# An expert's token tiles turned by VectorE in 32x32 blocks, after a load in 128-byte pieces, in place of two TensorE transposes

## The reference, cut to what matters

```
xn = layernorm(x)
# 1: attention over tokens (16 heads of 16 channels), then over channels
qk = (layernorm(xn, ln1) @ Wqk_t) in 16 heads;  v = ... @ Wv_t
attn = softmax(tau * (2 qk.qk' - |qk|^2 - |qk'|^2) / sqrt(16));  out = (attn @ v) @ Wo_t * gamma1
...                                   # channel attention on the result
# 2: a mixture of 8 experts, the best one for each token
h = relu(xn @ W1[e] + b1[e]);  y = h @ W2[e] + b2[e];  out = gate * y
result = x + (1) + (2)
```

## The kernel before, in words

| round | expert work on TensorE | name below |
|---|---|---|
| 0 | two transposes of the tile (x) | x round |
| 5, 10 | two transposes of the next tile, two last products with W2 of the one before | x+y round |
| 1, 6, 11 | two columns of h (W1 products), L1134 | h round |
| 2-4, 7-9, 12-14 | two columns of h, two products with W2 (y), L1118 | h+y round |
| 15 | two last products with W2 | y round |

## Time and profile before

### The profile page before, as it was taken

One profiled execution on the slowest core, in us unless ns is written; L12 is line 12 of the kernel. 1 busy time (PEld: TensorE's weight loads), 2 busy tenths in 40 slices (PEclk: granted clock), 3 DMA queues, 4 the chain that ended last, 5 costly groups with the idle time before them and its releaser, 6 DMA issues. The chain is left out here.

```text
span 1476.7 us, 27029 instructions
## 1 busy us (share of the span) xinstructions
PE 1391.3 (94%) x9041; PEld 663.7 (45%) x9041; DVE 403.0 (27%) x1009; ACT 1064.6 (72%) x1183; POOL 232.2 (16%) x314
## 2 busy tenths in 40 slices
PE   6997999999999999999999999999999999999978
PEld 4752222234444444444444444344444444444867
DVE  6872110011111211112111111111121111123977
ACT  4657999987777777777777777777777777775122
POOL 5210730001001000010010100100001001001870
PEclk9998999999999999999999999999999999999989
DMA  4686442724543626345454454353544645532423
GB/s 165 232 239 215 127 89 54 224 37 115 157 112 123 145 85 170 98 110 167 104 163 114 110 155 116 130 127 87 154 122 105 171 104 157 136 133 84 152 89 115
DMA packets 125321, 195.38 MB, mean 132 GB/s; under 512 B 22336, under 2 KB 91648, under 8 KB 121824
## 3 DMA queue, kind: packets, MB, share of 16 engines
q1 hardware_dynamic: 116240, 177.12, 44.0%
q0 software_dynamic: 9040, 17.71, 4.4%
HBM read 154.63 MB, written 35.95 MB: 129 GB/s over the span
## 5 line engine op out<-in xcount | busy, mean ns | idle before, releaser
L939 ACT ACTIVATE shared<-ps 128x1024 f32<-128x1024 f32 x1024 | 980.5, 1024 | 264.8 <-PE ps L1076 263.8
L1091 PE MATMUL ps<-shared,work 128*17 128x512 f32 x4096 | 505.6, 603 | 0.0
L1076 PE MATMUL ps<-mov,stat 52*128 52x512 f32 x2048 | 423.7, 465 | 51.3 <-ACT shared L939 37.4
L1076 PEld LDWEIGHTS ps<-mov,stat 52*128 52x128 f32 x2048 | 167.5, 185 | 428.4 <-ACT shared L939 402.4
L984 DVE TENSOR_SCALAR work<-ps,work 128x128 f32<-128x128 f32 x312 | 109.6, 351 | 587.2 <-PE ps L1134 572.3
L1091 PEld LDWEIGHTS ps<-shared,work 128*17 128x17 f32 x4096 | 90.1, 97 | 220.8 <-issue 199.2
L1134 PE MATMUL ps<-work,XNW 128*128 128x128 f32 x1248 | 180.7, 288 | 0.0
L1134 PEld LDWEIGHTS ps<-work,XNW 128*128 128x128 f32 x1248 | 151.0, 191 | 57.0 <-issue 57.0
L1118 PE MATMUL ps<-XNW,work 128*128 128x256 f32 x624 | 161.8, 382 | 0.0
L788 POOL DMA_DIRECT2D y_slots<-work x39 | 21.9, 562 | 701.2 <-DVE work L976 642.2
L1118 PEld LDWEIGHTS ps<-XNW,work 128*128 128x128 f32 x624 | 106.5, 191 | 12.8 <-issue 4.8
(11 more groups left out here) (170 smaller groups left out, 689.7 us busy)
## 6 DMA issues: line engine op xcount, KB each, us to landing
XNW<-in_L_ffn_W_dram SPq DMA_DIRECT2D x78, 1024.0 KB, 7.1
stat<-q_parts SPq DMA_DIRECT2D x192, 128.0 KB
mov<-q_parts SPq DMA_DIRECT2D x192, 64.0 KB
xg<-in_L_attn_x_dram SPq DMA_DIRECT2D x16, 512.0 KB, 4.9
q_parts<-XNW SPq DMA_DIRECT2D x16, 512.0 KB, 5.8
x_slots<-work SPq DMA_DIRECT2D x1, 4992.0 KB, 16.4
early<-x_slots SPq DMA_DIRECT2D x39, 128.0 KB, 2.2
early<-in_L_ffn_b_dram SPq DMA_DIRECT2D x39, 128.0 KB, 8.1
```

Source lines behind the costliest of these rows:

```text
L939: nc.scalar.activation(probs[:, s % DEEP, half * 1024:(half + 1) * 1024], ps[:, 2 * half:2 * half + 2].rearrange("p a b -> p (a b)"), ACT. ...
L1076: last = nc.tensor.matmul(ps[:, 2 * half + r], stat[rows, hh, m * P:(m + 1) * P], mov[rows, hh, half * 512:(half + 1) * 512], start=True, ...
L1091: last = nc.tensor.matmul(ps[32 * j:32 * j + VW, AV], Vh[:, hh, m], probs[:, s % DEEP, j * 512:(j + 1) * 512], start=(m == 0), stop=(m == ...
```

## The change

The tokens of a tile are no longer loaded as 128 rows of 1024 bytes. Four DMAs take them in pieces of 32 fp32 (128 bytes): DMA a fills the partitions 32a to 32a+31, and it picks the channels so that a transpose of each 32x32 block by itself gives the full transpose of the tile. This block transpose is one VectorE instruction on 128x256, from `xs` to `xsT`, both in SBUF. The two transposes on TensorE and the two copies on VectorE are gone, with their two uses of the ring: the pair now has 24 of these, not 30. A new semaphore `x_turned` tells TensorE that `xsT` is there, in front of the first h columns, and the wait on `tile_loaded` moves there as well; VectorE waits on `tile_loaded` too. A tile now takes 8 DMAs on SP's queue, not 5.

```diff
-        TILE_DMAS = 5
+        TILE_DMAS = 8
+        QUADS = 4
+        QUAD = P // QUADS
...
-                rounds[at] += [("x", tt, 0), ("x", tt, 1)]
+                rounds[at].append(("x", tt, 0))
...
-                    get(xs[:, tt], x_slots[bass.ds(n * P, P), :])
+                    rows = x_slots[bass.ds(n * P, P), :].rearrange("(t c) (k a r) -> a c k t r", c=QUAD, k=KC, r=QUAD)
+                    for a in range(QUADS):
+                        get(xs[a * QUAD:(a + 1) * QUAD, tt].rearrange("c (k t r) -> c k t r", k=KC, t=QUADS), rows[a])
...
+                            elif kind == "x":
+                                dve.wait_ge(tile_loaded[a], 16 * TILE_DMAS * (i - FIRST + 1))
+                                nc.vector.transpose(xsT[:, a].rearrange("p c n -> p (c n)"), xs[:, a]).then_inc(x_turned, 1)
...
-                                if kind == "x":
-                                    nc.vector.tensor_copy(xsT[:, a, b], ps[:, bank(k), 0:P]).then_inc(ring_taken, 1)
...
+                    if kind == "x":
+                        return
                     k = use[u]
                     at_least(pe, ring_taken, ring_base(i) + k - 1)
-                    if kind == "x":
-                        if b == 0:
-                            pe.wait_ge(tile_loaded[a], 16 * TILE_DMAS * (i - FIRST + 1))
-                        nc.tensor.transpose(ps[:, bank(k), 0:P], xs[:, a, b * P:(b + 1) * P],
-                                            ident[:, :]).then_inc(ring_ready, 1)
-                    else:
-                        if b == 0:
-                            pe.wait_ge(ring_taken, ring_base(i) + use[("x", a, 1)] + 1)
...
+                    if b == 0:
+                        pe.wait_ge(tile_loaded[a], 16 * TILE_DMAS * (i - FIRST + 1))
+                        pe.wait_ge(x_turned, 3 * (i - FIRST) + a + 1)
```

More of the change, by code:

```diff
@@ L738, in build @@
         ring_taken = sem("ring_taken")
+        x_turned = sem("x_turned")
         y_ready = sem("y_ready")
@@ L744, in ring_base @@
         def ring_base(i):
-            return 30 * (i - FIRST)
+            return 24 * (i - FIRST)
         def expert_plan():
@@ L762, in use_numbers @@
                 for u in uses:
-                    if u[0] != "y":
+                    if u[0] == "h":
                         table[u] = k
@@ L980, in expert_body @@
                                 dve.wait_ge(ring_ready, ring_base(i) + k + 1)
-                                if kind == "x":
-                                    nc.vector.tensor_copy(xsT[:, a, b], ps[:, bank(k), 0:P]).then_inc(ring_taken, 1)
-                                else:
-                                    nc.vector.tensor_scalar(hT[:, b], ps[:, bank(k), 0:P], b1s[:, a, b:b + 1], 0.0,
-                                                            ALU.add, ALU.max).then_inc(ring_taken, 1)
+                                nc.vector.tensor_scalar(hT[:, b], ps[:, bank(k), 0:P], b1s[:, a, b:b + 1], 0.0,
+                                                        ALU.add, ALU.max).then_inc(ring_taken, 1)
                         if n == 0:
@@ L1122, in expert @@
                         return
+                    if kind == "x":
+                        return
                     k = use[u]
                     at_least(pe, ring_taken, ring_base(i) + k - 1)
-                    if kind == "x":
-                        if b == 0:
-                            pe.wait_ge(tile_loaded[a], 16 * TILE_DMAS * (i - FIRST + 1))
-                        nc.tensor.transpose(ps[:, bank(k), 0:P], xs[:, a, b * P:(b + 1) * P],
-                                            ident[:, :]).then_inc(ring_ready, 1)
-                    else:
-                        if b == 0:
-                            pe.wait_ge(ring_taken, ring_base(i) + use[("x", a, 1)] + 1)
[L1133 to L1136, removed]
+                    if b == 0:
+                        pe.wait_ge(tile_loaded[a], 16 * TILE_DMAS * (i - FIRST + 1))
+                        pe.wait_ge(x_turned, 3 * (i - FIRST) + a + 1)
+                    for c in range(KC):
+                        last = nc.tensor.matmul(ps[:, bank(k), 0:P], w1s[:, a, c, b * P:(b + 1) * P],
+                                                xsT[:, a, c], start=(c == 0), stop=(c == KC - 1))
+                    last.then_inc(ring_ready, 1)
                 def expert_body(i, last_one=False):
```

## The result

The changed kernel takes 1481.42 us (median of 12 runs, 1478.39 to 1483.71), the kernel before 1477.94 us (12 runs on the same chip, 1475.30 to 1479.13). The ratio is 1.0027, with an interval of 1.0018 to 1.0036: slower by about 0.27%; the medians are 3.5 us apart. The time is within the range, but the likeliest case, 1479 us with no added falls of the clock, did not come. What came is the first rival, between its small size (1 to 3 more falls) and its full one (six), together with a gain that stood in no case.

A forecast was written before the change was run, and what follows sets the result against it. Light rounds were taken as bound by the chain of logits and ScalarE's exponentials, not TensorE; TensorE, VectorE, waits, DMAs and clock each added 0 to 1478.41 us, giving 1479 us, range 1476 to 1489.

The forecast's parts named there:

- the likeliest case: Whole kernel: removed TensorE work is off the path and no clock falls are added; 1479 us, chance 0.53.
- the first rival: In x rounds, less TensorE work makes the clock fall more often: about 1483 us to 1488.5 us; chance 0.39.
- the clock term: In x rounds of the expert pairs: 0 more clock falls, cost 0; up to nine more, 14.8 us, kept for the range.
- The bound of the light rounds: In x, y, h and x+y rounds, logits and ScalarE's exponentials set the length, about 4.8 us; removing transposes gains 0.
- the 17.2 us: TensorE's transposes in 13 x and 26 x+y rounds, 39 x 0.44 us, all predicted to be off the path.
- One of its signs: In the profile after, TensorE's busy time would be down by about 17 us at the same span.
- VectorE and the new wait: Block transposes of 0.43 us replace VectorE's copies, and TensorE's wait for `x_turned` in rounds 1, 6, 11 is covered; cost 0.
- The DMAs: Three more SP issues per tile and tokens landing in 5 us stay within 26 us of slack; cost 0.
- the doubled allowance: On SP's queue, loads going out 0.8 to 1.3 us later, with double allowed for pieces of 128 bytes.
- The forecast's test: Fallen x rounds in the profile after: three to five if the clock is right, seven or more if the prediction is wrong.
- The rival's full size: If transposes count in full for the clock, some six of nine kept pairs fall in their x rounds: 1488.5 us.

The follow-up runs named there:

- e1: The changed kernel with two TensorE transposes of the identity put back into the x round, results unread; 1474.35 us, ratio 0.9972 to the kernel before.
- e3: The changed kernel with one plain matmul of 128 columns added in the x round, result unread; 1474.23 us, ratio 0.998 to the kernel before.
- e6: The kernel before with its tiles loaded by the four DMAs in 128-byte pieces, TensorE transposes kept; ratio 1.0005 to the kernel before.
- e9: The kernel before with 4 small dead VectorE memsets at the start of the third stage; 1474.86 us, ratio 0.9978 to the kernel before.
- e4: The changed kernel with two plain one-column matmuls added in the x round, results unused; ratio 1.002 to the kernel before.
- e7: The changed kernel with the kernel before's one contiguous DMA per tile, block transpose kept; ratio 1.002 to the kernel before.
- e8: The changed kernel with 8 small dead VectorE memsets at the start of the third stage; ratio 1.0023 to the kernel before.
- e11: The changed kernel with 12 small dead VectorE memsets at the start of the third stage; 1482.97 us, ratio 1.0031 to the kernel before.
- e12: The changed kernel run once more, unchanged, beside another run on one chip; 1482.01 us, ratio 1.0029 to the kernel before.

## Why the prediction was right and wrong

The number came out near the forecast, 1481.4 against 1479, but not for the forecast's reason: the clock term was wrong, and an unforeseen gain of 3.7 us elsewhere hid half to three quarters of a second-stage loss of 5.0 to 7.4 us. That the time lies within the case's own range (1476.5 to 1481.5) is luck.

**The bound of the light rounds: right.** Where the clock holds, the rounds are as long without the transposes to 0.01 us, and none of the 17.2 us came off the path. One of its signs missed: TensorE's busy time is down by 4.5 us and not 17 (1391.3 to 1386.8), in good part because other groups grew as the transposes went and the clock fell more often: the values from 505.6 to 509.9 us, the W2 products from 161.8 to 164.5 and the logits from 423.7 to 425.3.

**VectorE and the new wait: right.** 0.43 us was taken for the block transpose, 0.424 is the mean, and it never waits. TensorE waits for none.

**The DMAs: right, with one term too small.** Each of the four small loads lands 2.2 us after its issue; issued one after another over 2.9 us, the tile's tokens are in about 4.5 us after the first issue (an estimate: 2.90 - 0.58 + 2.2), and 5 were taken. An issue on SP takes 0.58 us each and not 0.26 to 0.43, so a tile's first DMA and its stack's last lie 13.96 us apart (566.96 - 553.00) where it was 11.29: 2.7 us later, the doubled allowance. The next reload is at 590.31, so 23 us of slack are left.

**The clock: wrong.** The failed step is "I take 0 more falls, because the busy time of a window that fell is no lower than that of one that did not". That fallen and kept rounds had the same work (0.95 us busy in the same window of both; the 1.07 and 0.99 of the earlier trace rows differ only by where their windows begin) shows that the work of before stood at the edge; it says nothing on less work. It spoke for the rival. Measured: 4 falls before and 3 in e1, e3, e6 and e9, all with two transposes or as much in the x round; 8 or 9 in after, e4, e7, e8, e11 and e12, which lack them; 0 with more. The price, 1.64 us, holds for a fall that covers the values whole. Where it comes later in the round (3.0 us and more behind its first exponential, not 2.4 to 2.9) it is 1.1 to 1.5, so eight falls cost 11.5 us and not 13.1.

The Trainium skill's sentence on transposes, in "TensorE: Matmul & The Clock Gate", Part 4, isn't borne out for these fp32 transposes: by it e1 would have fallen as often as after, and it fell as seldom as e3.

**The forecast's test was sound.** "Three to five" falls was its sign, "seven or more" its refutation; eight came. The rival's full size was six of nine kept pairs; by the counts it is four or five more.

**The term that stood nowhere: the third stage.** The prediction looked only where instructions change. The third stage's own code is the same, but VectorE's gap in it is gone. The sum as it came: before 1477.9; more falls, +5.0 us by after's profile (four more) and +7.4 by e12's (five more); -3.7 us in the third stage; that gives 1479.2 to 1481.6, against 1481.4 and 1482.0 measured. Without this luck the change would have cost 7 to 8 us (3.5 or 4.3, and 3.7), where the rival's six falls gave 9.8.

**What stays open.** Why the gap of VectorE stands where it stands, and whether it is a wait for instructions; the theory by length agrees with e9 and e11, and not with e8. Why one pair of 13 falls and the next doesn't with the same work; that the fallen pairs come four apart before, and that the fall slides through the round from pair to pair after, points to the moment in the round and not to chance, but no run moved that moment by itself. How the transposes of the 26 x+y rounds would do alone wasn't tried; no fall was seen in those rounds in any kernel.

## What to carry to other kernels

Work that is hidden behind another engine isn't free to remove: on TensorE it may be what holds the clock. Before taking some away, look for the emptiest stretch in which the clock already falls now and then. If there is one, its work is at the edge: less of it brings more falls, more of it fewer. There, a matmul whose result nobody uses, laid into the hole, is worth more than the edit itself: 13.2 us on the changed kernel here and 5.8 us on the one before, at 0.02 us of length in the round as TensorE's starts have it. And a difference of a few tenths of a per cent has to be looked for in every stage, since a gap of 0.3 us in code that nobody had touched was worth 3.7 us.

## What the runs showed of the hardware

- Two fp32 transposes of 128x128 and one plain matmul of 128 columns hold TensorE's clock alike (3 falls of 13 each, e1 and e3; 8 and 9 with neither); two one-column matmuls with full weight loads don't (8, e4), though the trace has them busy for 0.61 us, the transposes for 0.44.
- The clock fell from 2.4 to 1.2 GHz with no idle stretch of TensorE longer than 0.97 us in the x round (0.59 in the kernel before).
- A multiplication of 32x64 on VectorE took 2.34 us, eleven times its 0.21, when GpSimd's of 128x1024 had begun 0.07 us earlier. A gap of 0.28 us had put it there. One that had begun 0.08 us before GpSimd's kept its 0.22 us, and the instruction behind it took 2.46 us and not 0.49.
- A 32 KB load in 256 pieces of 128 bytes landed in 2.2 us, as the 128 KB load in 128 pieces of 1 KB did; its issue on SP took 0.58 us against 0.33 to 0.37.
